# A gated delta-rule block: the triangular inverse by substitution on VectorE up to blocks of 16, and six weight pieces split in a later stage

## The reference

```python
M = tril(-(wk_scaled @ wk.T) * L_mask, -1)
A = solve_triangular(eye - M, eye, lower=True, unit_diagonal=True)   # (1 - M)^-1
intra = tril(rk @ wk.T * L_mask, -1)
v_new = A @ v_scaled - A @ wk_scaled_dec @ S
o     = rk_decay @ S + intra @ v_new
S     = chunk_end_decay * S + wk_pos @ v_new
```

## Time and profile before

| | us |
|---|---|
| median of 3 runs | 2561.7 (2559.56 to 2564.49) |
| the profiled execution | 2558.84 |
| its span, first to last instruction | 2557.1 |
| stage A, to the units' first transposes | 486.9 |
| TensorE busy | 2461.3 (96%) |
| VectorE busy | 1972.1 (77%) |
| ScalarE busy | 1645.3 (64%) |
| GpSimd busy | 1189.9 (47%) |

### The profile page before, as it was taken

One profiled execution on the slowest core, in us unless ns is written; L12 is line 12 of the kernel. 1 busy time (PEld: TensorE's weight loads), 2 busy tenths in 40 slices (PEclk: granted clock), 3 DMA queues, 4 the chain that ended last, 5 costly groups with the idle time before them and its releaser, 6 DMA issues.

```text
span 2557.1 us, 40983 instructions
## 1 busy us (share of the span) xinstructions
PE 2461.3 (96%) x14724; PEld 2060.9 (81%) x14724; DVE 1972.1 (77%) x3028; ACT 1645.3 (64%) x2578; POOL 1189.9 (47%) x758
## 2 busy tenths in 40 slices
PE   6999999999999999999799999999999999999997
PEld 4999999899999999988576777767777687776876
DVE  6776676555665666577798998989989889898996
ACT  5455554444444444566678778787787777877774
POOL 2224565100000000541576776767767577676774
PEclk9999999999999999999899999999999999999999
DMA  4456554344434434452464655646556456565563
GB/s 158 166 193 176 176 165 141 121 154 146 140 128 155 145 130 156 154 180 84 150 213 154 195 194 183 204 157 196 192 188 202 150 196 206 176 197 159 190 207 113
DMA packets 229609, 427.60 MB, mean 167 GB/s; under 512 B 24897, under 2 KB 112641, under 8 KB 229394
## 3 DMA queue, kind: packets, MB, share of 16 engines
q1 hardware_dynamic: 223250, 407.98, 48.6%
q0 software_dynamic: 6144, 16.79, 1.9%
HBM read 347.58 MB, written 77.10 MB: 166 GB/s over the span
## 4 chain that ended last, share of the span: by engine, by line
PE 69%; DVE 16%; ACT 7%; issue 6%; POOL 1%; DMA 1%; DVEq 0%; POOLq 0%; SPq 0%; ACTq 0%
PE pb L1350 14%; PE pb L1328 14%; PE pb L820 10%; DVE pb L1796 9%; PE pb L2100 4%; PE pb L2105 4%; PE pb L1999 4%; DVE UU L1802 3%; PE pb L812 2%; PE pb L2068 2%; PE pb L2126 2%; PE pb L2024 2%; PE pb L2082 2%; PE pb L2087 1%; PE pb L2015 1%
## 5 line engine op out<-in xcount | busy, mean ns | idle before, releaser
L1728 POOL TENSOR_TENSOR UU<-dx,BB 128x1024 f32<-128x1024 f32 x256 | 608.3, 2391 | 266.1 <-PE pb L1999 266.0
L1927 ACT ACTIVATE pb<-dt,al 128x512 f32<-128x512 f32 x512 | 341.5, 685 | 198.9 <-DVE UU L1802 197.7
L1255 DVE TENSOR_TENSOR HL<-HF,HH 128x512 fp32r<-128x512 f32 x248 | 171.6, 692 | 277.4 <-ACT HH L1170 277.3
L1166 ACT ACTIVATE HF<-pb,BU 128x512 f32<-128x512 f32 x248 | 170.5, 687 | 325.1 <-PE pb L1328 325.0
L1802 DVE TENSOR_TENSOR UU<-pb,CC 128x512 f32<-128x512 f32 x512 | 351.3, 686 | 19.4 <-DMA CC<-bcd 1.4
L1796 DVE TENSOR_TENSOR_SCAN pb<-pb,hs,UU 128x512 f32<-128x512 f32 x256 | 328.4, 1283 | 33.1 <-POOL UU L1728 11.7
L1796 DVE TENSOR_TENSOR_SCAN pb<-pb,UU 128x512 f32<-128x512 f32 x256 | 312.7, 1221 | 42.7 <-ACT pb L1927 28.6
L1129 POOL DMA_INDIRECT ya<-yg,sl x32 | 36.6, 1144 | 605.9 <-DMA yg<-YO 562.4
L1350 PE MATMUL pb<-W2h,HH 128*128 128x256 f32 x992 | 287.1, 289 | 0.0
L1999 PEld LDWEIGHTS pb<-ident,UU 128*128 128x128 f32 x2048 | 236.9, 143 | 59.6 <-issue 43.0
L1350 PE MATMUL pb<-W2l,HH 128*128 128x256 f32 x992 | 280.3, 283 | 0.0
(11 more groups left out here) (301 smaller groups left out, 5141.2 us busy)
## 6 DMA issues: line engine op xcount, KB each, us to landing
WH<-fhd SPq DMA_DIRECT2D x176, 512.0 KB, 3.6
BB<-bcd SPq DMA_DIRECT2D x256, 256.0 KB, 4.8
CC<-bcd SPq DMA_DIRECT2D x256, 256.0 KB, 4.7
raw<-in_w1a SPq DMA_DIRECT2D x23, 1024.0 KB, 5.0
raw<-in_w2a SPq DMA_DIRECT2D x23, 1024.0 KB, 7.7
xg<-zt SPq DMA_DIRECT2D x23, 512.0 KB, 6.0
TM<-xg SPq DMA_DIRECT2D x23, 512.0 KB, 8.7
yg<-YO SPq DMA_DIRECT2D x23, 512.0 KB, 3.1
```

The source lines that it names most:

```text
L1166: e.activation(HF[q % 2][:], wbank("h", q)[:], ACT.Silu, bias=BU[i][:, it:it + 1]).then_inc(s_hf, 1)
L1255: e.tensor_tensor(HH[q % 4][1][:], HF[q % 2][:], HH[q % 4][0][:].bitcast(F32), ALU.subtract).then_inc(s_hl, 1)
L1728: e.tensor_tensor(ubuf(n)[:], dx[p][:], BB[n % 4][:].rearrange("p (a m) -> p a m", a=1).to_broadcast([P, 2, 512]), ALU.mult).then_inc(p_u. ...
L1927: e.activation(abank(n, c)[:], dt[p][:, c, :], ACT.Exp, scale=al1[:, 2 * p + c, s:s + 1]).then_inc(c_a.sem, 1)
```

## The change

In stage A:

- The inverse of the diagonal 16x16 blocks is made by forward substitution on VectorE (`solve`): 31 small instructions a chunk on 128 x (8 x up to 15), for all 64 blocks of a chunk at once (partition = block row group and column, free = head, sequence and row), each waiting for the one before. For it, SP stores the diagonal blocks of M to DRAM (8 DMAs, 16 partitions x 8 runs of 64 bytes) and loads them back broadcast over the 16 partitions of each block (8 DMAs, `blocks`). `inverse` spreads the result by a block mask into `DT`, its transpose `d4` becomes `Dm`, and doubling goes on from level 4. Levels 1 to 3 and `seed` are gone.
- The order of all engines is written anew: `kk`, `M` and `MT` of the next chunk are made within this chunk, `v` and `kq` of the next one behind `vn` and `S`; the first 12 of the 31 instructions stand ahead of the state update and 19 behind it.
- `decay` on VectorE is gone; ScalarE makes the clipped differences with Relu and a bias (`lower`, `upper`, four instructions per head each). GpSimd's `Ea` is made in place.
- Two pieces of the gate's weights are split beside each chunk (16 in all, `NCA`) instead of three; the other six beside units 1 to 6 (`weights`: unit 1 has piece 16, unit 6 piece 21), in buffers of their own. `flag` is made in unit 8 and 9, on a bank of the rotation.
- 16 of the zero stores to `xg` go beside the layer norm, the rest three per chunk.
- The first unit's weights are split behind the last piece, at the end of stage A.

Core of the diff (`...` marks what is left out):

```diff
+NCA = 16
...
-        order = ["kq", "P1", "t1", "D1", "v", "P2", "t2", "D2", "wkT", "P3", "t3", "D3", "wkS", "P4", "t4", "D4",
-                 "P5", "t5", "D5", "P6", "t6", "T6", "vn", "rkT'", "o", "kk'", "S", "MT'"]
+        ahead = ["rkT", "z", "kk", "MT", "v", "kq", "rkT'"]
+        order = ["kk'", "wkT", "d4", "wkS", "P4", "D4", "P5", "t5", "D5", "P6", "t6", "T6", "MT'", "vn", "rkT''", "v'", "o", "S", "kq'"]
...
         def sp_a(e):
+            def blocks(n):
+                for h in range(2):
+                    e.wait_ge(*g_dve[h].at("M", n))
+                for q in range(8):
+                    e.dma_start(md[n, 16 * q:16 * q + 16], M2[16 * q:16 * q + 16, :, :, 16 * q:16 * q + 16]).then_inc(s_md, 16)
+                e.wait_ge(s_md, 128 * (n + 1))
+                if n:
+                    e.wait_ge(*g_x.at(30, n - 1))
+                for q in range(8):
+                    e.dma_start(MB[16 * q:16 * q + 16].rearrange("p r g c -> p (r g c)"),
+                                md[n, 16 * q + 1:16 * q + 16].rearrange("(o r) h b c -> o (r h b c)", o=1).to_broadcast([16, 1920])).then_inc(s_mb, 16)
...
             for n in range(NSEQ):
+                if n + 1 < NSEQ:
+                    blocks(n + 1)
+                if n:
+                    halves(2 * n - 1)
+                    residuals(n - 1)
+                if n + 2 < NSEQ:
+                    sums(n + 2)
+                zeros(*range(16 + 3 * n, min(19 + 3 * n, NU)))
...
+                halves(2 * n)
...
         def pool_a(e):
             for n in range(NSEQ):
+                if n + 1 < NSEQ:
+                    upper(n + 1)
+                scatter(chunk_pairs(n, 0))
+                rest(2 * n)
+                scatter(chunk_pairs(n, 1))
+                if n + 2 < NSEQ:
+                    lower(n + 2)
+                if n + 1 < NSEQ:
+                    decayed(n + 1)
+                rest(2 * n + 1)
+                scatter(chunk_pairs(n, 2))
...
         def dve_a(e):
+            def solve(n, steps):
+                for k in steps:
+                    r = (k - 1) // 2
+                    if k == 0:
+                        e.wait_ge(s_mb, 128 * (n + 1))
+                        e.wait_ge(*a_dve.at("eye"))
+                        e.tensor_copy(X16[:], eye[:].rearrange("p (a r) -> p a r", a=1).to_broadcast([P, 8, 16])).then_inc(g_x.sem, 1)
+                        continue
+                    e.wait_ge(*g_x.at(k - 1, n))
+                    if k % 2:
+                        e.tensor_tensor(Y16[:, :, r:15], MB[:, r:15, :, r].rearrange("p r g -> p g r"),
+                                        X16[:, :, r:r + 1].to_broadcast([P, 8, 15 - r]), ALU.mult).then_inc(g_x.sem, 1)
+                    else:
+                        e.tensor_tensor(X16[:, :, r + 1:16], X16[:, :, r + 1:16], Y16[:, :, r:15], ALU.add).then_inc(g_x.sem, 1)
+            def inverse(n, h):
+                e.wait_ge(*g_x.at(30, n))
...
+                e.tensor_tensor(TB[h]["DT"][:].rearrange("p b (q r) -> p b q r", r=16),
+                                X16[:, 4 * h:4 * h + 4, :].rearrange("p b (a r) -> p b a r", a=1).to_broadcast([P, 4, 8, 16]),
+                                blk16, ALU.mult).then_inc(g_dve[h].sem, 1)
...
             for n in range(NSEQ):
+                if n:
+                    residual_a(n - 1)
+                if more:
...
+                        mix(n + 1, h)
...
+                for l in (4, 5, 6):
+                    level(l, n)
+                    routed(n, l - 1)
+                if n + 2 < NSEQ:
+                    norms(n + 2)
...
+                if more:
+                    for h in range(2):
+                        values(n + 1, h)
+                    solve(n + 1, range(12))
+                routed(n, 6)
...
+                if more:
+                    for h in range(2):
+                        inner(n + 1, h)
+                    solve(n + 1, range(12, 31))
+                    for h in range(2):
+                        inverse(n + 1, h)
...
         def act_a(e):
             for n in range(NSEQ):
+                copy("wk", n, "wkT", "wk")
+                copy("d4", n, "d4", "Dm")
+                if n:
+                    rest(2 * n - 1)
+                if more:
+                    upper(n + 1)
+                    decays(n + 1, "ET")
+                    decays(n + 1, "ez")
+                    carried(n + 1)
...
+                copy("t5", n, "t5", "DT")
+                copy("t6", n, "t6", "DT")
+                high(2 * n)
+                if more:
+                    copy("MT", n + 1, "MT", "MT")
                 copy("vn", n, "vn", "vn")
+                if n + 2 < NSEQ:
+                    turned_rows(n + 2)
+                rest(2 * n)
+                if n + 2 < NSEQ:
+                    lower(n + 2)
...
+                if n + 3 < NSEQ:
+                    for b in range(4):
+                        squares((n + 3 + 8 * b,))
+                    roots(n + 3)
+                high(2 * n + 1)
+            rest(NCA - 1)
+            for l in range(2):
+                e.wait_ge(s_w0, 32)
+                e.activation(WB[0][2 * l][:], fview[l], ACT.Copy).then_inc(s_w0h, 1)
...
         def sp_units(e):
+                if u - 1 in weights:
+                    q = weights[u - 1]
+                    e.wait_ge(s_chi, q + 1)
+                    e.dma_start(fhd[q], chi_b[:].bitcast(F32)).then_inc(s_cst, 16)
+                    e.wait_ge(s_clo, q + 1)
+                    e.dma_start(fld[q], clo_b[:].bitcast(F32)).then_inc(s_cst, 16)
+                    if q + 1 < NCH:
+                        e.wait_ge(s_cnt, q + 1)
+                        e.dma_start(craw_b[:], fch[q + 1]).then_inc(s_craw, 16)
...
         def act_units(e):
+                if u in weights and it == 2:
+                    c = weights[u]
+                    e.wait_ge(s_craw, 16 * (c + 1))
+                    e.wait_ge(s_cst, 32 * c)
+                    e.activation(chi_b[:], craw_b[:], ACT.Copy).then_inc(s_chi, 1)
```

More of the change, by code:

```diff
@@ L199, in program @@
         for h in range(2):
[L200 removed]
+            us = [(k.rstrip("'"), k.count("'")) for k in ahead]
             for m in range(NSEQ):
[L202 removed]
+                us += [(k.rstrip("'"), m + k.count("'")) for k in order + ["y"] if m + k.count("'") < NSEQ]
             if h == 0:
@@ L602, in dve_a, with level @@
                     (2, 1): 10, (2, 2): 11, (2, 3): 12, (2, 4): 13}
-            decay(0)
             for h in range(2):
                 mix(0, h)
-                seed(0, h)
-            for n in range(NSEQ):
+            norms(1)
+            for h in range(2):
+                values(0, h)
+            for h in range(2):
+                inner(0, h)
+            solve(0, range(31))
+            for h in range(2):
+                inverse(0, h)
+            def level(l, n):
                 for h in range(2):
@@ new lines, in sums_of, with await_sums, lower @@
+            def sums_of(n, h):
+                return ZR[h] if n else gbank("z", 0, h)[:].rearrange("p (b m) -> p b m", b=4)
+            def await_sums(n, h):
+                if n:
+                    e.wait_ge(s_zr, 16 + 32 * n)
+                else:
+                    e.wait_ge(*g_pe[h].at("z", 0))
+            def lower(n):
+                for h in range(2):
+                    W, z_ = TB[h], sums_of(n, h)
+                    await_sums(n, h)
+                    if n:
+                        e.wait_ge(*g_dve[h].at("M", n - 1))
+                    for b in range(4):
+                        t = e.activation(W["E"][:, b, :], z_[:, b, :], ACT.Relu, bias=sm["ncum"][:, n + 8 * b, h:h + 1])
+                    t.then_inc(g_act[h].sem, 1)
@@ new lines, in roots, with high, rest @@
+            def roots(n):
+                e.wait_ge(s_sq, 8 * n + 8)
+                e.activation(rn[:, n:NT:8, :], rn[:, n:NT:8, :], ACT.Sqrt).then_inc(s_rnq, 1)
+            def high(c):
+                e.wait_ge(s_craw, 16 * (c + 1))
+                if c:
+                    e.wait_ge(s_cst, 32 * c)
+                e.activation(chi[:], craw[:], ACT.Copy).then_inc(s_chi, 1)
+            def rest(c):
+                e.wait_ge(s_clo, c + 1)
+                e.activation(craw[:], clo[:].bitcast(F32), ACT.Abs, accum_out=cnt[:, c:c + 1]).then_inc(s_cnt, 1)
@@ L1016, in program @@
         LB = NU + NB - 1
+        weights = {u + 1: NCA + u for u in range(NCH - NCA)}
+        UF = NCH - NCA + 2
         front_pe = {**{(LB - 4 + c, 3): [("in", 0, c)] for c in range(4)}, (LB, 5): [("xp", 0, 0)], (LB, 6): [("dt", 0, 0), ("dt", 0, 1)]}
```

503 lines of the change are left out of this document (277 added, 226 removed).

## The result

| | us |
|---|---|
| kernel before, 20 runs | 2561.35 (2555.36 to 2566.3) |
| changed kernel, 20 runs | 2567.69 (2561.93 to 2571.76) |
| ratio | 1.0024, 95% interval 1.0017 to 1.0031 |
| changed kernel, profiled execution; its span | 2569.8; 2568.1 |

The change makes the kernel 6 us slower; forecast were 53 us less. On another chip the same kernel gave 1.0036 (1.0024 to 1.0049).

A forecast was written before the change was run, and what follows sets the result against it. TensorE's instruction stream was taken to bound both the delta-rule stage and the units. -70.9 + 4.5 + 11.9 + 1 = -53.5 us from 2558.8 gives 2505.3, with 2.9 for the median 2508 (2490 to 2518; 8 in 10: 2474 to 2542).

The forecast's parts named there:

- seven periods: Delta-rule stage, from first to last `vn`: 41.0 us each plus 15 for routing, 302 against 372.9, so -70.9 us.
- So the solve is just covered: After TensorE's last S product, VectorE's 7.5 us up to the first `inverse` lie beside 8.0 us of TensorE's work.
- 2.5 of blocking: GpSimd's rkdT and clo block VectorE during the last 19 operations and `inverse`: 0 to 5.1 us a period, half taken.
- rival 4: The small operations of `solve` are slow, at 0.6 us each 11 us more a chunk: 2596 us, slower than before; chance 0.04.
- Rival 3: SP's order bounds: ScalarE's high half waits for a late craw load, period 44.5, chunk 0 +9: 2537 us; chance 0.14.
- The removal and TensorE's bound: Levels 1 to 3 go from TensorE, 13.3 us a chunk; a clean period bound by TensorE alone falls from 50.8 to 37.5.
- The price of a free small operation: VectorE's substitution: 0.18 us fixed and 1 ns an element, 7.6 us a chunk, 3.4 for the first 12 operations.
- Routing: In the first chunks VectorE also does the routing: 15 us on the path, bounds 8 and 15.7.
- Chunk 0: Nothing covers the blocks' round trip there: first `vn` at 104.1 instead of 99.6, +4.5 us, bounds -2 and +13.
- Tail: From the last `vn` to the units, weight splits come behind the last piece: 26.3 us instead of 14.4, +11.9, bounds +5 and +15.
- Units: Weight splits beside routed units fit into ScalarE's and GpSimd's idle time, TensorE stays at 100%: +1 us, 0 to 6.

The follow-up runs named there:

- e9b: Changed kernel with ScalarE's high half of a chunk's first weight piece behind the MT and vn copies; run twice, ratios 0.9982 and 0.9988 of the kernel before.
- t1b: Changed kernel with the blocks' DRAM round trip in chunk 0 only, 12 small operations ahead of `values`, rk on ScalarE; 2525.31 us, ratio 0.9872 in the second run.
- e8: Changed kernel with GpSimd's scatters moved: one pair of tiles behind the first piece's subtraction, three behind the second's; 2538.66 us, ratio 0.9922 of the kernel before.
- c3b: Changed kernel with reordered engines, scatters and loads, rk on ScalarE, 15 weight pieces beside chunks and seven beside units; 2495.98 us, ratio 0.9757 of the kernel before.
- e4: Changed kernel with the first unit's weights split behind piece 14 instead of piece 15; 2559.44 us, ratio 1.0007 of the kernel before.
- c3: The same kernel as c3b, run on a slower chip; ratio 0.9837 of the kernel before.

## Why the prediction was wrong, step by step

The term that failed is that of the seven periods: 7 x 41.0 + 15 = 302 us forecast, 357.2 measured, 55 of the 65 us. One step in it is wrong, and a loop and a term are missing; the first three of these points tell them.

- **"So the solve is just covered", 7.5 us against 8.0, and 2.5 of blocking.** This step failed. From the S operations to the end of the first `DT` VectorE needed 14.8 us (219.2 to 234.0). 6 of the 7 too many are blocking: not 2.5, and more than the upper bound of 5.1, because only rkdT and clo were placed there. GpSimd's selects and products, which I named under rival 4 and dismissed as few, fall there too. The Trainium skill, page "SBUF — State Buffer", section "SBUF: two separate sides", has the shared port as an exclusive lock; the ends that coincide to 0.1 us agree, and the rule should have been applied to every GpSimd operation of the chunk that reads SBUF. One more us is that eight S operations stood there and not four.
- **The missing loop.** I took each engine's work as something that TensorE covers and never closed the loop from M to the next M. Rival 3 had its mechanism and 0.14 of the chance, with 16.3 us from M to craw's landing; it was 21: 12.3 to the issue (forecast 11.6) and 8.7 to land (4.7). That landing was taken from a profile without the round trip; with it the median is 8.9, and in e3, which leaves the round trip out of chunks 1 to 7, it is 4.0. Even so rival 3 was only half. With craw's part of the loop cut the period stayed (e9b), since the sums' load stands in the same queue; with both loads early it stayed too (e3), since the loop through rk, v and the substitution is as long. Only with that one shortened as well did the third and the fourth come to 41.9 (t1b), and a part of that is the hold of GpSimd, which fell elsewhere. How the gain is shared between the loops and the hold stays open.
- **Scatters.** No term at all: 26 to 29 us. GpSimd's scatter was moved ahead of the subtraction, and SP's reloads behind `blocks`; both stand in the diff, and the price of 1.27 us an indirect write stands in the trace of before. The wait for rows doesn't: before, GpSimd never waits for them, in the changed kernel 68.1 us in three waits, and in e8, which only moves the scatters, 17.1 in two. What stands behind a moved line on its in-order queue was not followed to its end.
- **The removal and TensorE's bound.** Right: the levels' instructions are gone, and c3b's periods of 39.5 without routing come near 37.5. The price of a free small operation was right as well (12 in 3.7, forecast 3.4).
- **Rival 4.** Its outcome came, a kernel slower than before, and so did its sign: the small operations average 0.44 and 0.45 us in the third and fourth period, over 0.4 and close to its break-even of 0.46 (0.35 over all chunks). Its cause was not the stride, since a free operation costs what was forecast; it was the blocking, against which the prediction had set "so few can be blocked". It had 0.04 of the chance, and forecast 2596.
- **Routing.** 15 us forecast. c3b's two routing periods exceed its next two by 8.3 and 6.7, 15 in all. In the changed kernel they exceed them by 3.7 in all, as other loops hold the next two there, so the term can't be read in it.
- **Chunk 0.** +8.9 instead of +4.5, inside its bounds. The blocks landed at 77.3, 1.2 us later than the sum has it: the eight stores took 5.5 us to issue instead of 3.2, and the last of them had landed within 2 us instead of 4, where 3 more had been held possible. The 31 operations took 10.3 us (77.3 to 87.6) instead of 7.6, two of them blocked by GpSimd, and level 4's P began at 93.4 instead of 85.6, behind d4 and wkS (which this sum lacks), TensorE's granted clock being 0.60 on average from 77 to 90; from there to `vn` it went 3 us faster than forecast.
- **Tail.** 28.3 forecast as 26.3: 5.4 us behind GpSimd's last operation instead of the 2 of the earlier trace rows, partly made up by a craw load that landed in 3.6.
- **Units.** Right: TensorE at 100%. Some 2.5 us more behind them were not looked into.

Of the 65 us, then: scatters 27, by experiment; the tied loops with the lock in them some 28, which is what is left of the 55; chunk 0 and tail 6.5; the rest 3.

## What to carry to other kernels

When a change takes work off the engine that bounds, write the loop that remains as one sum, from a value to the same value of the next stage, through every queue on the way; "covered by the other engine" is a check of one segment and says nothing of the loop. If two single fixes give nothing, cut both before giving up the theory, and then read what else the joint cut has moved before crediting the theory with all of the gain. And follow each moved line on the in-order queues to what stands behind it: here the place of the scatters on GpSimd cost as much as half of the expected gain.

## What the hardware showed that was not expected

- A DMA's issue on SP isn't of one price: the stores of 64-byte runs (16 partitions, 8 KB) took 0.60 each, a 120 KB load 0.42, the `rows` loads 2.35 each and one `fhd` store 4.67 us. The profile doesn't say why.
- At the end of the stage 5.4 us lay between GpSimd's last operation and TensorE's first of the units, which waited for GpSimd's queue (in e4 as well, 483.0 to 488.4).
- A VectorE operation of 0.2 us with two SBUF inputs took 0.5 to 2.2 us where a GpSimd operation ran, selects included, and ended within 0.1 us of it. A chain of small dependent operations paid for most of what GpSimd did beside it: the 19 were 6.0 us longer for 8.1 us of GpSimd's.
- Two of the chips ran the kernel before in 2601.7 and 2601.4 us, against 2557.5 to 2561.4 on the others. The same kernel (c3 there, c3b here) had there waits on three engines that the profile ascribes to nothing, some in the units too; TensorE's and ScalarE's in the window 60 to 1100:
```profile
PE pb L1004 <- issue: 31.8, 5, 8.4
...
ACT DT L907 <- remote: 30.6, 6, 8.7
ACT HF L1398 <- remote: 22.1, 2, 12.1
```
against
```profile
PE pb L1004 <- issue: 3.0, 2, 1.5
```
The ratios carry over badly as well (c3 0.9837 there, 0.9757 here). Their cause stays open.
